# The transposed row maxima are moved into the packed queries by GpSimd's queue in place of SyncE's

## The reference

```
q, k, v = proj(w_q, b_q), proj(w_k, b_k), proj(w_v, b_v)      # (B, H, T, dk)
scores  = einsum('bhtd,bhsd->bhts', q, k) / sqrt(dk)
attn    = softmax(scores)
out     = einsum('bhts,bhsd->bhtd', attn, v)
y       = einsum('btd,ed->bte', out.transpose(0, 2, 1, 3).reshape(B, T, D), w_o) + b_o
```

## Time and profile before

| | |
|---|---|
| median of 3 runs | 526.82 us |
| lowest, highest | 524.11, 530.07 us |
| span of the profiled execution | 525.4 us |
| its busy shares | TensorE 90%, VectorE 77%, ScalarE 71%, GpSimd 43% |
| granted TensorE clock, mean | 0.987 of full speed |

### The profile page before, as it was taken

How to read it: one execution, slowest core, us unless ns; L and a number is a source line. 1 busy time by engine, 2 the same in 40 slices (tenths; PEclk the granted TensorE clock), 3 DMA queues, 4 the chain that set the end, 5 groups by cost and what they waited for, 6 DMA issues and landing times.

```text
span 525.4 us, 11035 instructions
## 1 busy us (share of the span) xinstructions
PE 472.5 (90%) x3416; PEld 276.7 (53%) x3416; DVE 404.0 (77%) x1063; ACT 372.3 (71%) x739; POOL 228.4 (43%) x544
## 2 busy tenths in 40 slices
PE   2458998998999999888899899999999999999994
PEld 1212454544544455444346576666666666666662
DVE  4688898989999999768926859788687959687453
ACT  2315887878989988767684576886868696867551
POOL 6054333325444635221003453938567483716241
PEclk9999999999999999989899999999999999999998
DMA  6443334444444433330023353535444644535431
GB/s 197 134 137 109 118 111 133 127 135 132 122 143 142 134 115 105 119 116 29 3 88 120 118 168 97 189 109 178 141 145 161 179 168 122 194 105 192 133 128 40
DMA packets 51737, 67.48 MB, mean 128 GB/s; under 512 B 4192, under 2 KB 35168, under 8 KB 51680
## 3 DMA queue, kind: packets, MB, share of 16 engines
q1 hardware_dynamic: 51680, 66.78, 41.1%
HBM read 51.17 MB, written 15.20 MB: 126 GB/s over the span
## 4 chain that ended last, share of the span: by engine, by line
PE 59%; SPq 12%; DVE 9%; issue 8%; ACT 5%; DMA 5%; POOL 1%; POOLq 0%; DVEq 0%; ACTq 0%
PE pY L1385 8%; PE pS L1385 8%; SPq L408 6%; PE pS L1369 6%; PE pS L1370 6%; PE pS L1371 6%; PE pO L1304 5%; PE pS L1248 5%; SPq L396 4%; DVE mneg L923 4%; DMA k_scratch<-k_parts 2%; DMA qp<-mT 2%; ACT probs L703 2%; PE pS L1254 2%; SPq L416 2%
## 5 line engine op out<-in xcount | busy, mean ns | idle before, releaser
L923 DVE TENSOR_REDUCE mneg<-pS 128x2 f32<-128x512 f32 x256 | 163.7, 684 | 25.0 <-PE pS L1248 24.5
L703 ACT ACTIVATE probs<-pS 128x512 f32<-128x512 f32 x256 | 144.0, 595 | 29.8 <-PE pS L1254 28.2
L1248 PE MATMUL pS<-kp,qp 48*128 48x256 bf16 x512 | 87.4, 290 | 24.4 <-DVE mneg L923 9.3
L789 ACT ACTIVATE h_ring<-r 128x512 f32<-128x512 f32 x104 | 65.0, 625 | 35.0 <-DVE r L1092 26.2
L1369 PE MATMUL pS<-qp,up_hi 128*128 128x512 f32 x144 | 89.3, 620 | 0.0
L1254 PE MATMUL pS<-qp,kp 51*128 51x256 bf16 x512 | 87.1, 281 | 0.9 <-ACT probs L703 0.7
L1304 PE MATMUL pO<-probs,vv 128*32 128x256 f32 x1024 | 74.5, 398 | 0.4 <-ACT oT_sb L655 0.4
L1248 PEld LDWEIGHTS pS<-kp,qp 48*128 48x128 bf16 x512 | 34.2, 96 | 74.8 <-DVE mneg L923 42.4
L1092 DVE SCALAR_TENSOR_TENSOR r<-pS,probs 128x512 f32<-128x512 f32 x64 | 43.4, 686 | 22.2 <-PE pS L1371 21.7
L1092 DVE SCALAR_TENSOR_TENSOR r<-pS,c_ring 128x512 f32<-128x512 f32 x64 | 44.0, 687 | 17.8 <-PE pS L1371 15.4
L1370 PE MATMUL pS<-kp,up_hi 128*128 128x512 f32 x144 | 57.1, 396 | 0.0
(11 more groups left out here) (193 smaller groups left out, 855.5 us busy)
## 6 DMA issues: line engine op xcount, KB each, us to landing
c_ring<-c_scratch SPq DMA_DIRECT2D x32, 512.0 KB, 4.0
probs<-c_scratch SPq DMA_DIRECT2D x32, 512.0 KB, 4.2
qp<-q_scratch SPq DMA_DIRECT2D x64, 96.0 KB
kp<-k_scratch SPq DMA_DIRECT2D x64, 96.0 KB
q_scratch<-q_parts SPq DMA_DIRECT2D x16, 192.0 KB, 2.4
k_scratch<-k_parts SPq DMA_DIRECT2D x16, 192.0 KB, 2.6
q_scratch<-q_parts SPq DMA_DIRECT2D x16, 128.0 KB, 2.6
k_scratch<-k_parts SPq DMA_DIRECT2D x16, 128.0 KB, 2.3
```

What stands on the lines that cost most here:

```text
L703: nc.scalar.activation(probs[j][:, hh], pS2[n % S2_RING][:, :, :], ACT.Exp, scale=SCALE).then_inc(exp_done, 1)
L789: nc.scalar.activation(h_ring[:, (n - at) % HRING], r_sb[n % URING][:, :], ACT.Square).then_inc(sq_done, 1)
L923: nc.vector.tensor_reduce(mneg[u % 2][:, :, hh, k], pS1[n % S1_RING][:, :].rearrange("p (a s) -> p a s", a=TH), AX.X, ALU.max, negate=True ...
L1248: return mm(pS1[n % S1_RING][:, T * th:T * (th + 1)], qp[slot][rows, k, P * th:P * (th + 1)], kp[slot][rows, k, :], start=True, stop=True)
```

## The change

load_max moves from the SyncE program to the GpSimd program. For each unit it now stands behind split_max(u) and behind what follows it there (for unit 0 part3(2) and chain_x(1), for unit 27 the split of the down weights, for even units norm_x, part2 and part3), and ahead of chain_y, residual1 and chain_x1. It waits for the kept maxima as before, and newly for the slot of the ring to be free, which SyncE's order gave before. The two transfers, their shapes and their semaphore are the same.

```
@@ SyncE
-            def load_max(u):
-
-                sp.wait_ge(mT_kept, u + 1)
-                for hh in range(2):
-                    at, n = HALF * hh + QK_ROWS, M_ROWS * UB
-                    sp.dma_start(qp[u % RING][at:at + M_ROWS], mT_sb[u % 2][n * hh:n * (hh + 1), :]
-                                 ).then_inc(m_packed[u % RING], 16)
...
             write_parts(2)
-            load_max(0)
             load_unit(4)
-            load_max(1)
...
                     write_parts(b + 3)
-                if 2 * b + 2 < NU:
-                    load_max(2 * b + 2)
                 if 2 * b + 6 < NU:
                     load_unit(2 * b + 6)
-                if 2 * b + 3 < NU:
-                    load_max(2 * b + 3)
@@ GpSimd
+            def load_max(u):
+
+                pool.wait_ge(mT_kept, u + 1)
+                if u >= RING:
+                    pool.wait_ge(s2_done, TH * UB * (u - RING + 1))
+                for hh in range(2):
+                    at, n = HALF * hh + QK_ROWS, M_ROWS * UB
+                    nc.gpsimd.dma_start(qp[u % RING][at:at + M_ROWS], mT_sb[u % 2][n * hh:n * (hh + 1), :]
+                                        ).then_inc(m_packed[u % RING], 16)
...
                         part3(nc.gpsimd, pool.wait_ge, u // 2 + 2)

+                load_max(u)
                 for i in range(2):
                     if u == 2 * PREP[i] + 3:
                         chain_y(i)
```

## The result

| | before | after |
|---|---|---|
| median | 526.38 us (14 runs) | 522.80 us (14 runs) |
| lowest, highest | 522.36, 530.80 | 520.65, 525.10 |
| ratio | | 0.9934, 95% interval 0.9908 to 0.996 |
| span of the profiled execution | 525.4 us | 520.0 us |
| TensorE waits for qp from mT | 6.4 us | none |

The kernel became 3.6 us faster (0.66%). Forecast were plus 0.6 us: the amount is inside the range, the direction is not.

A forecast was written before the change was run, and what follows sets the result against it. TensorE, 90% busy, was taken as the engine to look at, waiting 6.4 us for maxima queued on SyncE. Losses of 6.96 us less the 6.4 us gain gave plus 0.6 us, 527.4 us; range 521.5 to 532.5 us.

The forecast's parts named there:

- 6.4 us put in: Attention: TensorE's six waits for packed query rows from mT were all taken as gone, minus 6.4 us.
- The size of d: Time one transfer holds GpSimd: SyncE's 0.75 us issue plus a 0.22 us small operation, so 0.97 us.
- the prediction's own formula: Net change in time as 8d - 7.2 us, d being the time one transfer holds GpSimd.
- The likeliest case: Whole kernel: gain and losses cancel to within 1%, d between 0.24 and 1.56 us; 527.4 us, chance 0.60.
- The four losses: GpSimd's uncovered places, the start and three statistics chains: 1.94 + 1.87 + 1.55 + 1.60 = 6.96 us lost.
- start: Unit 0's pair sits between GpSimd's long chain and split_max(1), delaying TensorE's transpose by 1.94 us.
- unit 13: chain_y(0) on GpSimd comes later behind this unit's pair, so ScalarE waits 1.55 us.
- unit 17: chain_x1(0) on GpSimd comes later behind this unit's pair, so ScalarE loses 1.60 us.
- unit 19: chain_y(1) on GpSimd comes later behind this unit's pair, so ScalarE waits 1.87 us.
- Nearly free: Rival: issue on GpSimd costs a small operation, d 0.22 us, deciding below 0.24; minus 5.4 us, 521.4 us, chance 0.15.
- slow: Rival: GpSimd's issue is slow, d about 1.8 us, deciding from 1.56; plus 7.2 us, 534.0 us, chance 0.25.
- the upper bound: d on GpSimd at most 1.5 us, twice what SyncE needs for the same transfer; 531.6 us at that end.

The follow-up runs named there:

- the odd units behind the chains: Against the kernel before: only odd units' load_max moved to GpSimd, placed behind chain_y, residual1 and chain_x1; 521.25 us, ratio 0.9903; repeated, 521.81 us.
- the run with four transfers: Changed kernel with each transfer of the maxima cut in two, so GpSimd issues four for a unit; 540.17 us, 1.0289 of the kernel before.
- the run with odd units only: Against the kernel before: odd units' load_max moved to GpSimd ahead of the chains, even units left on SyncE; 523.53 us, ratio 0.9960.

## Why the prediction was wrong

**The views and the gain.** The waits for qp from mT went from 6.4 us to none, and the pair of an even unit does stand right behind k_parts, as foreseen. The gain of the move by itself was 7.71 us by the traces of before and of the odd units behind the chains, near the 6.4 us put in. It stands in the six blocks that had a wait: 1.25, 0.77, 0.60, 0.34, 2.27 and 2.50 us, behind waits of 1.17, 0.55, 0.55, 0.28, 2.19 and 1.69 us. Most of what exceeds the waits is in the last of them, where the clock fell behind the wait in the kernel before:

```profile
228.00:231.00 3.00, 1.31 (x18) 0.92 (x14) 1.62 (x3) 1.86 (x5) 0.89 (x4) 1.00 0.16 43
231.00:234.00 3.00, 3.00 (x35) 1.14 (x34) 1.76 (x3) 1.84 (x4) 0.00 (x0) 0.60 0.35 100
```

So the sum was nearly right; what made the maxima late was not. The prediction has it that they stand behind load_unit and write_parts, and says: "That a shorter queue gives more than these waits I count at nothing: its other transfers are not what TensorE waited for." With only the even maxima moved they were (7.2 us of waits behind the start), and with the odd ones moved alone the even ones, in their old place, were late no more but for one wait of 1.1 us. The gap at 198.90 to 200.52 in the earlier trace rows had been read rightly, and not carried to its end: a queue that is never idle but for a landing is the limit, whoever is late. For the change as made, where both pairs leave, this cost the forecast little.

**The size of d.** This is the step that failed. 0.97 us was taken, by the argument that an engine's own program should not be faster than SyncE's 0.75 us; 0.556 us was measured. By the prediction's own formula that is 8 x 0.556 - 7.2 = minus 2.8 us, 524.1 us, the right direction. The likeliest case as it was bounded, d between 0.24 and 1.56 us and a change of less than 1%, is the one that came; the value taken inside these bounds gave the wrong sign. The four losses, each at the measured d, against the trace:

| | by the formula, d = 0.556 | measured |
|---|---|---|
| start | 1.11 | 1.12 (TensorE's wait) |
| unit 13 | 0.72 | 0.90 |
| unit 17 | 0.77 | 0.88 |
| unit 19 | 1.04 | 1.13 |

The places and the mechanism were right; measured are the waits in the changed kernel. What they cost in block time is less, 2.16 us for the three. The start's 1.1 us can be seen in block 1's o_rec too, which varies by itself: it came at 63.78 to 66.02 us in the seven traces with unit 0 on SyncE and at 65.53 to 66.41 in the four with it on GpSimd, 64.98 and 66.13 on average. One reading was wrong without harm: a wait of ScalarE for nm was "0.7 us at most" before, but there is one of 1.07 us, at 303.80 among the experts.

**What was missing.** The end: 1.9 us that come with 64 transfers of GpSimd and were in no part of the sum. It happens to make up for the gain being larger: by the terms as measured, 0.9 (ahead of block 1) + 2.2 + 1.9 - 7.7 = minus 2.7 us, where the medians say minus 3.6, with an interval from minus 4.8 to minus 2.1. That these two partly cancel is luck.

**The rivals.** "Nearly free" asked for d below 0.24, "slow" for 1.56 and more: neither. The rule of the Trainium skill, "DMA: Bandwidth & Descriptors", in the section on the anatomy of one DMA on the gpsimd path, that descriptor generation is small against the fixed 2 us, agrees in tendency: 0.556 us to issue, 2.3 us from issue to landing. The other, from the Trainium skill, "SBUF — State Buffer", the box on the DVE blocking DMA, is that VectorE's two-port operations hold up the writing of descriptors. Whether that happened here is not shown: the longest of 64 issues was 0.787 us at a median of 0.556, and the longest landing 5.1 us at a median of 2.3. TensorE waited for none of these landings. For the upper bound the run with four transfers is a warning: the straight line from d to time did not hold at twice the holding time, where the clock fell behind each of the three longer waits and the end grew.

## What to carry to other kernels

A queue whose only idle time is the wait for its own transfers to land is a bound, even if the waits that it causes look like the fault of a single late transfer; to know which of its transfers is dear, ask which lies beside the landing (free) and which does not. Moving a small transfer to another engine costs that engine's time at every place where something urgent is behind it, so put the move behind the urgent work, and move only as many as are needed. A cost that no row of the old trace shows is better measured first by itself than taken from the engine that did it before: here the new engine was the faster one.

## What the runs showed of the hardware

GpSimd issues a transfer of 6 KB in 0.556 us, SyncE the same one in 0.752 us. With many such transfers the end of the kernel grows by 0.081 us for each beyond some 40 (62 to 128 were measured, and 0, 30 and 32, where it does not).

A wait can be followed by a fall of the clock. In the run with odd units only, TensorE was busy for 2.04 of 3 us in the stretch in which ScalarE waited for the third chain, and was granted 0.61 of its clock soon after, a mix of its two levels, 2.4 and 1.2 GHz:

```profile
174.00:177.00 3.00, 2.04 (x28) 0.85 (x28) 2.32 (x5) 1.86 (x5) 2.69 (x9) 1.00 0.38 142
...
180.00:183.00 3.00, 3.00 (x25) 1.16 (x25) 1.84 (x4) 2.12 (x5) 0.66 (x3) 0.61 0.68 202
```

That block took 15.74 us, 0.55 us more than the same block in the first trace of the changed kernel, which had the same wait and no fall. The second trace of the changed kernel had the fall too (0.50 at 180 to 183 us, a block of 15.66 us), so the fall comes in one execution of the same kernel and not in another. In the kernel before, the wait of 1.69 us was followed by one and the longest, of 2.19 us, by none. It is why single spans differ by more than the terms above: the 12 blocks of the changed kernel took 168.44 us in one trace and 169.60 in the other.

The granted clock that the record gives for the start is no guide to the speed there. For 13 to 58 us the record of before says full speed:

```profile
13.00:58.00 45.00, 30.04 (x183) 12.14 (x184) 34.77 (x76) 18.31 (x42) 14.10 (x35) 1.00 0.42 125
```

and that of after about half:

```profile
13.00:58.00 45.00, 29.27 (x177) 11.80 (x178) 34.10 (x76) 17.42 (x40) 17.73 (x41) 0.54 0.43 130
```

TensorE's busy time is nearly the same, 30.04 and 29.27 us, and so are its single products, 0.61 us for four at 31.08 us before and at 30.84 us after. The second trace of the changed kernel has 1.00 for this stretch, with 29.20 us busy.
